# Row maxima finished once per group, a block row split 384+256, and a tangent product moved to the end of a list

## What is computed

```python
def _L0_attn_ref(x, Wq, bq, Wk, bk, Wv, bv, Wo, bo, J_attn, lambda_attn):
    Q, K, V = heads(Wq, bq), heads(Wk, bk), heads(Wv, bv)      # [b, 16, 1024, 16]
    scores = jnp.einsum('bhid,bhjd->bhij', Q, K) / scale
    QJ = jnp.einsum('bhid,hde->bhie', jnp.tanh(Q), J_attn)
    delta = jnp.einsum('bhie,bhje->bhij', QJ, jnp.tanh(K))
    scores = scores + lambda_attn * delta
    scores = jnp.where(causal, -jnp.inf, scores)
    probs = jax.nn.softmax(scores, axis=-1)
    out = jnp.einsum('bhij,bhjd->bhid', probs, V)
    ...
x = x + 0.5 * ffn(layernorm(x))
x = x + attn(layernorm(x))
x = x + 0.5 * ffn(layernorm(x))
```

## Time and profile before

| | us |
|---|---|
| runs of the kernel before | 1605.68, 1595.5, 1597.59 |
| their median | 1597.59 |
| span of the profiled execution | 1576.1 |
| first maximum unit of the opening | 494.1 |
| first score of group 0 | 547.67 |
| a plain group (961.2 to 993.3) | 32.1 |
| two hosting groups (592 to 671) | 79.0 |

### The profile page before, as it was taken

One profiled execution on the slowest core, in us unless ns is written; L12 is line 12 of the kernel. 1 busy time (PEld: TensorE's weight loads), 2 busy tenths in 40 slices (PEclk: granted clock), 3 DMA queues, 4 the chain that ended last, 5 costly groups with the idle time before them and its releaser, 6 DMA issues. The chain is left out here.

```text
span 1576.1 us, 25755 instructions
## 1 busy us (share of the span) xinstructions
PE 1439.2 (91%) x8992; PEld 1095.1 (69%) x8992; DVE 1022.7 (65%) x2609; ACT 712.3 (45%) x1117; POOL 684.3 (43%) x650
## 2 busy tenths in 40 slices
PE   4699999999877599999999999999986999999998
PEld 3589988989765355555555555555555888989997
DVE  7855665655386677776777778887367566565554
ACT  5333333333232156666666666666563333333332
POOL 1375556564524433333333331323403655656643
PEclk9799999999988699999999999999987999999999
DMA  9444443442378926666666668672064444345422
GB/s 307 131 106 98 94 88 64 92 101 28 67 216 201 316 76 169 168 169 169 169 168 169 154 169 242 161 218 100 29 204 148 101 96 87 67 94 101 93 37 25
DMA packets 125720, 208.61 MB, mean 132 GB/s; under 512 B 24424, under 2 KB 86376, under 8 KB 122536
## 3 DMA queue, kind: packets, MB, share of 16 engines
q1 hardware_dynamic: 88984, 160.06, 35.3%
q0 software_dynamic: 30720, 38.46, 14.9%
q10 hardware_dynamic: 5904, 8.66, 1.9%
HBM read 126.36 MB, written 84.64 MB: 134 GB/s over the span
## 5 line engine op out<-in xcount | busy, mean ns | idle before, releaser
L2089 ACT ACTIVATE a_wts<-a_s_psum 128x1024 f32<-128x1024 f32 (+1 forms) x384 | 301.0, 809 | 183.9 <-PE a_s_psum L2221 181.9
L1964 DVE CUSTOM_DVE_ANT_0 a_m_psum<-a_m_psum,mask 128x128 f32<-128x128 f32 (+1 forms) x492 | 238.7, 501 | 130.2 <-PE a_m_psum L2187 122.5
L2187 PE MATMUL a_m_psum<-a_kp,a_qp 96*128 96x512 f32 (+2 forms) x737 | 272.2, 398 | 20.5 <-DVE a_parts L1964 6.5
L2187 PEld LDWEIGHTS a_m_psum<-a_kp,a_qp 96*128 96x128 f32 x737 | 140.0, 192 | 130.1 <-DVE a_parts L1964 52.5
L1913 POOL TENSOR_SCALAR_AFFINE_SELECT a_wts<-a_wts 128x512 f32<-128x512 f32 x128 | 78.4, 637 | 328.0 <-ACT a_wts L2089 328.0
L1032 ACT ACTIVATE e_act_a<-e_a_psum 128x512 f32<-128x512 f32 (+1 forms) x192 | 101.2, 527 | 259.9 <-PE e_a_psum L1109 259.9
L2221 PE MATMUL a_s_psum<-a_qp,a_kp 97*128 97x512 f32 (+2 forms) x768 | 210.6, 356 | 0.4
L243 POOL DMA_INDIRECT e_slots<-normalized,e_token x160 | 168.7, 1054 | 81.7 <-issue 47.2
L949 DVE TENSOR_TENSOR e_hid<-e_act_a,e_g_psum 128x512 f32<-128x512 f32 (+1 forms) x192 | 114.5, 596 | 131.8 <-PE e_g_psum L1109 127.5
L1128 PE MATMUL e_o_psum<-e_w_hi,e_h_hi 128*128 128x256 f32 x640 | 183.2, 286 | 0.0
L890 POOL DMA_INDIRECT out<-e_res,e_sum_row x80 | 126.5, 1581 | 126.6 <-ACT e_res L1044 113.5
(11 more groups left out here) (292 smaller groups left out, 2757.3 us busy)
## 6 DMA issues: line engine op xcount, KB each, us to landing
packs<-x_res SPq DMA_DIRECT2D x48, 512.0 KB, 5.9
e_w_raw<-in_W_in SPq DMA_DIRECT2D x16, 1024.0 KB, 6.7
a_qp<-packs SPq DMA_DIRECT2D x15, 1024.0 KB, 8.1
a_kp<-packs SPq DMA_DIRECT2D x15, 1024.0 KB, 14.0
e_w_raw<-in_W_out SPq DMA_DIRECT2D x16, 512.0 KB, 8.6
normalized<-r_xn SPq DMA_DIRECT2D x16, 512.0 KB, 4.6
packs<-q_pack SPq DMA_DIRECT2D x16, 512.0 KB, 6.8
a_qp<-packs SPq DMA_DIRECT2D x16, 512.0 KB, 10.1
```

The source lines that it names most:

```text
L1964: nc.vector.tensor_tensor_reduce(products, products, c["mask"][:, QC - width:], 1.0, MASKED, ALU.add, ALU.max, top).then_inc(max_read, 1)
L2089: nc.scalar.activation(wts[(u * NS + s) % 2][:, j, 0:w], s_ps[q % 2][:, 0:w], ACT.Exp).then_inc(weighed, 1)
L2187: nc.tensor.matmul(m_ps[bank((n, h, z))][:, 0:stream], qp[n % NB][0:PACK, h, qt * P:(qt + 1) * P], kp[n % NB][0:PACK, h, part * QC:part * ...
```

## The change

Three edits. (1) The finish, transpose, negation and row transfer are done once per group, for four heads together: the parts of a group lie in one tile of 128 x 4 x 8 x 2, `top_of` reduces it to 128 x 32 before DVE reads the third unit of the next group, PE transposes 32 columns, ACT negates 32 x 128 and sends one row of 4 x 1024. The waits of DVE for its own results go. The transpose stands where that of the fourth head stood. The first score of a group waits for the whole row; later scores wait for none. (2) Units carry their first key block and their number of blocks; the fifth block row is 384 + 256 instead of 512 + 128. (3) The second tangent product of the opening moves from entry 42 to entry 58 of `EVENTS`; the list now has one transpose of group 0 where it had four.

```diff
-    UNITS = [(0, 0), (3, 0), (1, 0), (4, 0), (2, 0), (5, 0), (4, 1), (6, 0), (5, 1), (7, 0), (6, 1), (7, 1)]
+    UNITS = [(0, 0, 1), (3, 0, 4), (1, 0, 2), (4, 0, 3), (2, 0, 3), (5, 0, 4), (4, 3, 2), (6, 0, 4), (5, 4, 2), (7, 0, 4), (6, 4, 3), (7, 4, 4)]
...
-        parts = [sb(f"parts{u}", [P, KT, 2]) for u in range(2)]
-        tops = [sb(f"tops{u}", [P, KT]) for u in range(2)]
+        parts = [sb(f"parts{u}", [P, GH, KT, 2]) for u in range(2)]
+        tops = [sb(f"tops{u}", [P, GH * KT]) for u in range(2)]
...
-        row_in = kit.sems("a_row_in", "0 1 2 3")
+        row_in = kit.sem("a_row_in")
...
-            if k >= LAG and (k - LAG) % NU == NU - 1:
-                EVENTS.append(((k - LAG) // PER_GROUP, (k - LAG) % PER_GROUP // NU, None))
+            if k >= LAG and (k - LAG) % PER_GROUP == PER_GROUP - 1:
+                EVENTS.append(((k - LAG) // PER_GROUP, GH - 1, None))
...
-                    18: (("v", 2),), 21: (("v", 3),), 25: (("y", 1, 0),), 28: (("y", 1, 1),), 42: (("t", 1),)}
+                    18: (("v", 2),), 21: (("v", 3),), 25: (("y", 1, 0),), 28: (("y", 1, 1),), 58: (("t", 1),)}
...
+            def top_of(n):
+                dve.wait_ge(max_read, (n + 1) * PER_GROUP)
+                dve.wait_ge(turned, n + 1)
+                nc.vector.reduce_max(tops[n % 2][:], parts[n % 2][:].rearrange("p h t z -> p (h t) z"), AX.X).then_inc(topped, 1)
+
             def seen(n, h, z, at):
...
+                if n and (h, z) == (0, 2):
+                    top_of(n - 1)
...
-                if z == NU - 1:
-                    dve.wait_ge(max_read, m + 1)
-                    dve.wait_ge(turned, n * GH + h + 1)
-                    nc.vector.reduce_max(tops[h % 2][:], parts[h % 2][:], AX.X).then_inc(topped, 1)
-                    dve.wait_ge(topped, n * GH + h + 1)
+                if m == GROUPS * PER_GROUP - 1:
+                    top_of(n)
...
-                act.wait_ge(negated, n * GH + h + 1)
-                nc.scalar.dma_start(qp[n % NB][PACK:PACK + 1, h, :].bitcast(F32), neg[h % 2].bitcast(F32)).then_inc(row_in[h], 16)
+                act.wait_ge(negated, n + 1)
+                nc.scalar.dma_start(qp[n % NB][PACK:PACK + 1, :, :].rearrange("o h c -> o (h c)").bitcast(F32), neg[n % 2].bitcast(F32)).then_inc(row_in, 16)
...
-                width = (qt + 1) * P - part * QC if part or qt < 4 else QC
-                stream = max(width, 2 * P)
+                stream = max(tiles_in, 2) * P
...
-                nc.tensor.transpose(m_ps[bank((n, h, None))][0:KT, 0:P], tops[h % 2][:], c["ident"][:]).then_inc(turned, 1)
+                nc.tensor.transpose(m_ps[bank((n, h, None))][0:GH * KT, 0:P], tops[n % 2][:], c["ident"][:]).then_inc(turned, 1)
...
-                if s == 0:
-                    pe.wait_ge(row_in[j], (g + 1) * 16)
+                if q == 0:
+                    pe.wait_ge(row_in, (g + 1) * 16)
```

More of the change, by code:

```diff
@@ L1954, in add_bias @@
                                         bv[:].rearrange("p (g h c) -> p g h c", h=GH, c=HD), ALU.add).then_inc(v_read, 1)
+            def top_of(n):
+                dve.wait_ge(max_read, (n + 1) * PER_GROUP)
+                dve.wait_ge(turned, n + 1)
+                nc.vector.reduce_max(tops[n % 2][:], parts[n % 2][:].rearrange("p h t z -> p (h t) z"), AX.X).then_inc(topped, 1)
             def seen(n, h, z, at):
-                qt, part = UNITS[z]
+                qt, first, tiles_in = UNITS[z]
                 m = n * PER_GROUP + h * NU + z
+                if n and (h, z) == (0, 2):
+                    top_of(n - 1)
+                if n > 1 and (h, z) == (0, 0):
+                    dve.wait_ge(topped, n - 1)
                 dve.wait_ge(maxed, m + 1)
-                width = (qt + 1) * P - part * QC if part or qt < 4 else QC
-                top, products = parts[h % 2][:, qt, part:part + 1], m_ps[at][:, 0:width]
-                if (qt + 1) * P == part * QC + width:
+                width, part = tiles_in * P, min(first, 1)
+                top, products = parts[n % 2][:, h, qt, part:part + 1], m_ps[at][:, 0:width]
+                if qt + 1 == first + tiles_in:
                     kit.part(dve)
@@ L2026, in negate @@
             def negate(n, h):
[L2027 to L2032, removed]
+                act.wait_ge(turned, n + 1 + 2)
+                if n > 1:
+                    act.wait_ge(row_in, (n - 1) * 16)
+                nc.scalar.activation(neg[n % 2], m_ps[bank((n, h, None))][0:GH * KT, 0:P], ACT.Copy, scale=-1.0).then_inc(negated, 1)
             def row(n, h):
-                act.wait_ge(negated, n * GH + h + 1)
-                nc.scalar.dma_start(qp[n % NB][PACK:PACK + 1, h, :].bitcast(F32), neg[h % 2].bitcast(F32)).then_inc(row_in[h], 16)
+                act.wait_ge(negated, n + 1)
+                nc.scalar.dma_start(qp[n % NB][PACK:PACK + 1, :, :].rearrange("o h c -> o (h c)").bitcast(F32), neg[n % 2].bitcast(F32)).then_inc(row_in, 16)
             def take(g, ch):
@@ L2126, in was_read @@
                 if what == "turn":
-                    pe.wait_ge(negated, last[0] * GH + last[1] + 1)
+                    pe.wait_ge(negated, last[0] + 1)
                 elif what == "max":
```

10 lines of the change are left out of this document (4 added, 6 removed).

## The result

| | before | changed |
|---|---|---|
| median, runs taken side by side | 1603.66 us (1592.37 to 1608.32, 20 runs) | 1593.16 us (1585.45 to 1603.99, 20 runs) |
| ratio, 95% interval | | 0.9945 (0.9927 to 0.9964) |
| span of the profiled execution | 1576.1 us | 1584.6 us |

The ratio is that of the means: the change gains 0.55%, some 8.8 us, where 1.0% was forecast. The medians differ by 10.5 us. The forecast in microseconds stood on a median of 1597.59 us; beside the changed kernel the kernel before took 1603.66 us. On the old base the ratio gives 1588.8 us. So the 11 us by which 1593 lies above 1582 are 6 us of base and 5 to 7 us of missing gain (15.3 forecast, less 10.5 by the medians or 8.8 by the means).

What follows compares the result with a forecast made beforehand. PE and DVE were taken to wait for each other by turns, with the opening held by POOL. Opening 8.5 plus groups 6.8 gave 15.3 us off the profiled 1576.1; carried to the 1597.59 us median, 1582 us, range 1567 to 1592.

Steps and rivals of the forecast that it cites:

- The opening: End of the opening list: moving the second tangent product brings the first score from 547.67 to 539.2 us, gaining 8.5 us.
- PE's wait: In the opening, ahead of the second tangent product: PE's wait for POOL falls from 14.6 to 2 to 4 us.
- The plain groups: Groups hosting no projections: 0.3 us from finishing once plus 0.15 us from the split; about 31.6 us each.
- The single finish: Each group: three of four transposes leave PE, 0.3 us gained a group, bounds 0.1 and 0.6 us.
- the split: Each group, 384 + 256: PE streams 128 columns less a head, 0.15 us gained a group, bounds 0 and 0.25 us.
- DVE's relief: Each group: DVE is relieved by 1.3 us of finish work, valued at 0 because it is not on the path.
- 15 groups x (0.3 + 0.15 + 0) = 6.8 us: Loop total: transposes 0.3, split 0.15 and DVE's relief 0 us a group, taken for 15 groups.
- DVE as the bound: Rival, in the groups: DVE's relief counts, 22 us there, 30 us with the opening, 1567 us; chance 0.13.
- Late row: Rival: every group's first score waits for its row; 1629 us at a landing of 8.5 us; chance 0.14.
- near bound of 2.0 us: Row transfer in the groups: shortest landing time, from a store with idle DMA engines, against 5.4 us left before need.
- The clock stays up: Rival, end of the opening: a busier PE keeps 2.4 GHz, 2.5 us more gained, 1580 us; chance 0.04.
- Small opening: Rival: group 0's row holds the first score until 542.6 us, opening gains 5 us, 1591 us in all; chance 0.14.

Runs made afterwards that it cites:

- tangent_only: The kernel before with only the second tangent product of the opening list moved, from entry 42 to 61; ratio 0.9928 against the kernel before.
- hold3: The changed kernel with a projection's bank passed over for 3 places instead of 4; ratio 0.9861 against the kernel before.
- before_hold3: The kernel before with a projection's bank passed over for 3 places instead of 4; ratio 0.9987 against the unedited kernel before.
- hold_x2: The changed kernel with only the bank of a half's transposed x passed over for 2 places instead of 4; ratio 0.9916 against the kernel before.
- tangent_back: The changed kernel with the second tangent product put back from entry 58 to 40, ahead of max unit 40; ratio 1.0008 against the kernel before.
- hold3_last2: hold3 with the second tangent product at entry 60 instead of 58, second measurement, on another chip; ratio 0.9852, where the changed kernel had 0.9919.

## Why the prediction was right or wrong

**The opening: right.** The sum had 8.5 us; the profiles show 53.2 and 53.6 us against 44.2, 44.4 and 46.0, a gain of 7.2 to 9.4 us, and tangent_only (44.6) shows that all of it is the moved product. From the product to the first score it was 3.6 us, as forecast (539.2 - 535.55). The first score came 44.2 us after the first unit, against my 539.2 - 494.1 = 45.1; nearly all of the 0.9 us between them is chance, for the product itself started anywhere from 40.6 to 42.4 us after the first unit in the three profiles (41.5 us before). PE's wait fell to 4.8 us and not to 2 to 4. There the prediction disagrees with itself: its own 14.6 us less 17 units at 0.6 us leave 4.4 us.

**The plain groups: the total near, its parts not.** The sum had 0.45 us a group, the trace 0.30. The single finish gave 0.4 (my 0.3, put down to the transposes), the split cost 0.1 (I had 0.15 gained, and 0 as the lower bound: nothing excluded a loss, since the split also changes what DVE reads when; why it costs was not looked into). DVE's relief at 0 held in two plain groups of three and, within 0.2 us, at the reciprocals, where I had priced it at 0.39 us per us. There the single finish was worth 1.1 us; I had read the 33.6 us of that group as the price of DVE's work, and 1.1 us of its excess was had back without touching DVE's reciprocals.

**The step that failed** is "15 groups x (0.3 + 0.15 + 0) = 6.8 us". One plain group's term was multiplied by fifteen, and nine of these groups host projections. There I forecast 9 x 0.45 = 4.1 us; the undisturbed groups gave 4 x 0.16 - 5 x 0.19 = -0.3 us. The cause is shown by hold3 against before_hold3, and by hold_x2, where one number moved a wait from step 3 to step 7: a transpose taken out of a list changes which bank every later entry gets, and in the host groups the new order put units behind reads that come late. I had written that one bank of three is free for longer and counted that as a help. The bank rule was in the code, and the order of a host group could have been written out by hand for both kernels.

**The rest of the groups' term.** Undisturbed, groups 1 to 15 gave 2.1 us of 6.8. In the timed runs nothing is seen of them, twice, but 2 us are within those intervals, and nothing in tangent_back, whose opening was 1 us longer. The changed kernel's mean clock was 0.003 to 0.004 below that of the product alone, both times, but not below that of the kernel before; whether the clock ate the 2 us was not shown.

**The time.** The forecast of 1582 us was missed by 11 us, and 6 of them are the base: three runs with a median of 1597.59 us stood for a kernel whose twenty have 1603.66 us. That 1593 us lies above the range of 1567 to 1592 us at all is due to this base; the missing gain alone would have left it inside.

**The rivals.** DVE as the bound: excluded by the plain groups. Late row: excluded in the loop, where rows landed after 2.1 to 5.2 us in the three profiles of the changed kernel; beside a load that is 4.4 of 5.6 us, a thinner cover than the near bound of 2.0 us let it look. In the opening it was near: the row of group 0 took 5.0 to 9.3 us in them, and in hold3_last2 the first score stood for it. The clock stays up: no, in the changed kernel's profile it was at half from 532.7 to 553.1 us. Small opening: no. The gain that was eaten came from none of the four, and the order of the banks had no rival of its own. By the traces the sum would have been 8.5 + 2.1 = 10.6 us, a ratio of 0.993, the middle of the three that were measured for the changed kernel (0.9945, 0.9930, 0.9919).

## What to carry to other kernels

When an instruction is taken out of a list from which buffers are dealt in turn, write out for each kind of stage which buffer every later entry gets and whose read it then waits for; a saving read from the plainest stage holds for that stage only. Then retune the rule that deals them: one number was worth 0.7% once the list had changed, and nothing that the timing shows before. A rule that deals all later entries anew cannot be tuned at one place: hold_x2 mended step 3 and broke step 7. And compare stages of traces, not spans: code that was the same differed by 20 us between the two profiles.

## What the hardware showed that I had not expected

- Four chips ran the same code outside attention in 921 to 925 us on the first and in 942 to 956 us on the others (on one of these from 945 to 956 us, from profile to profile), more than the whole change is worth; only runs taken side by side on one chip can be compared.
- The granted clock fell to 1.2 GHz for 3.4 or 6.8 us in the middle of the loop in some executions and not in others, with the same instructions ahead of it, at 1.5 to 2.1 us each, in the even hosts and plain groups and never in an odd host; covering the longest pause did not end it.
- A small transfer of 16 KB took 2.1 us from issue to landing with the DMA engines 3 to 5% busy, 4.4 us beside a load that kept them 86.5% busy, and 4.8 to 9.5 us, differing from profile to profile, beside the loads of the opening.
